# TensorE's up projections first and down projections last in the wave steps, and nine dense chunks of the fifth group moved ahead

## What is computed

```python
def reference(x, ...):
    h = adapter(x, language)                    # small two-layer adapter and layer norm
    for i in range(4):                          # four Mamba layers
        n = layer_norm(h)
        xs, z = split(n @ W_in.T)
        u = silu(causal_conv4(xs) + cb)
        dt, B, C = split(u @ W_x.T);  dt = softplus(dt @ W_dt.T + b_dt)
        # for t:  state = exp(dt*A)*state + dt*B*u ;  y = sum over 16 states of state*C
        h = h + ((y + u * D) * silu(z)) @ W_out.T
    x = x + h
    # dense mixture: 8 experts and a shared one, every token through all nine
    m = (1 - sg) * sum_e gate_e * ((silu(x @ Wg[e]) * (x @ Wu[e])) @ Wd[e]) + sg * shared(x)
    # sparse mixture: top 2 of 8 experts by m @ wg, 1024 slots each, exact gelu
    return x + combine(dispatch(m))
```

## Time and profile before

| | us |
|---|---|
| median of 3 runs (2779.27 to 2789.38) | 2783.77 |
| profiled execution | 2781.01 |
| its span, first to last instruction | 2779.3 |
| iterations 0 to 14, from the first scan at 122.1 | 853 |
| iterations 15 to 30 | 1142.8 |
| iteration 31 and the end of the wave, to 2195.0 | 77 |
| dense phase, to TensorE's last down | 393 |

### The profile page before, as it was taken

The page is one execution under the profiler, slowest core; times in us unless marked ns, Lnnn a source line. Parts: engine busy times, 40 slices in busy tenths (PEclk is TensorE's granted clock), DMA queues, the critical chain, the costliest instruction groups (busy, mean ns, idle before and its releaser), DMA issues. The chain is left out here.

```text
span 2779.3 us, 22910 instructions
## 1 busy us (share of the span) xinstructions
PE 2392.7 (86%) x6062; PEld 1060.4 (38%) x6062; DVE 2064.0 (74%) x2022; ACT 1565.8 (56%) x2430; POOL 2048.5 (74%) x1268
## 2 busy tenths in 40 slices
PE   5389989989988889888898889888987799999586
PEld 3133333333333333333333333333332344444364
DVE  4389999999999988888888888888888433333221
ACT  2367776776777666666666666666664232322132
POOL 3379999999998878888888888888888422231176
PEclk9799999999999999999999999999998899999798
DMA  7444564455445766666666566666665500000154
GB/s 198 163 150 152 199 221 176 157 197 193 154 143 188 258 210 215 217 224 210 213 220 212 197 217 216 215 215 219 217 210 182 185 11 17 27 16 8 40 118 73
DMA packets 217995, 462.38 MB, mean 166 GB/s; under 512 B 29644, under 2 KB 111506, under 8 KB 217746
## 3 DMA queue, kind: packets, MB, share of 16 engines
q1 hardware_dynamic: 204178, 449.66, 48.4%
q0 software_dynamic: 11264, 7.98, 1.9%
q10 hardware_dynamic: 2432, 3.38, 0.3%
HBM read 437.51 MB, written 23.99 MB: 166 GB/s over the span
## 5 line engine op out<-in xcount | busy, mean ns | idle before, releaser
L831 DVE TENSOR_TENSOR_SCAN hh<-dA,psdB 128x1024 f32<-128x1024 f32 x512 | 1167.6, 2284 | 97.3 <-ACT dA L735 39.1
L906 POOL TENSOR_TENSOR gg<-hh,Clo 128x1024 f32<-128x1024 f32 x408 | 960.8, 2358 | 213.6 <-DVE hh L831 209.5
L556 PE MATMUL psY<-gg,ident 128*128 128x512 f32 x1708 | 877.3, 640 | 88.9 <-POOL gg L910 56.4
L735 ACT ACTIVATE dA<-dt,Acur 128x508 f32<-128x508 f32 x1024 | 664.7, 708 | 20.6 <-DVE hh L831 20.2
L556 PEld LDWEIGHTS psY<-gg,ident 128*128 128x128 f32 x1708 | 328.9, 202 | 546.9 <-issue 374.7
L820 DVE TENSOR_TENSOR psdB<-psT,Blo 128x1024 f32<-128x1024 f32 x395 | 483.2, 1223 | 59.8 <-ACT psT L706 44.6
L1296 DVE TENSOR_TENSOR ac<-sg,d_bank 128x512 f32<-128x512 f32 x144 | 99.0, 687 | 244.2 <-PE d_bank L1146 227.0
L537 PE MATMUL psW<-xnT,wcur 128*128 128x512 f32 x512 | 236.5, 604 | 39.2 <-ACT u L672 19.7
L906 POOL TENSOR_TENSOR gg<-hh,late 128x1024 f32<-128x1024 f32 x104 | 243.9, 2362 | 19.1 <-PE psY L556 18.9
L1195 ACT ACTIVATE sg<-d_bank 128x512 f32<-128x512 f32 x144 | 86.0, 597 | 262.1 <-PE d_bank L1142 262.1
L1050 POOL TENSOR_TENSOR xw<-x1T,wbc 128x512 f32<-128x512 f32 x36 | 37.5, 1044 | 257.0 <-PE d_bank L1146 244.1
(11 more groups left out here) (171 smaller groups left out, 2965.8 us busy)
## 6 DMA issues: line engine op xcount, KB each, us to landing
Blo<-rows SPq DMA_DIRECT2D x280, 512.0 KB, 5.3
Clo<-rows SPq DMA_DIRECT2D x280, 512.0 KB, 4.8
late<-rows SPq DMA_DIRECT2D x104, 512.0 KB, 7.8
wcur<-taps_l SPq DMA_DIRECT2D x32, 512.0 KB
disp<-fw SPq DMA_DIRECT2D x16, 528.0 KB, 8.3
dx<-disp SPq DMA_DIRECT2D x16, 528.0 KB, 6.3
fw<-in_Wg SPq DMA_DIRECT2D x32, 256.0 KB, 5.1
fw<-in_Wu SPq DMA_DIRECT2D x32, 256.0 KB, 4.9
```

The source lines that it names most:

```text
L556: ins = pe.matmul(psY[:, :], lhsT=ident[:, :], rhs=gg[k % NGB][:, j, :], start=False, stop=(k % NK == NK - 1 and j == last - 1))
L735: ins = act.activation(dA[k % NDA][:, j, :, 1:T], dt[i % 2][:, c, :, 1:T], ACT.Exp, scale=Acur[i % 2][:, s:s + 1])
L831: dve.tensor_tensor_scan(out=hh[k % NHB][:, :, :].rearrange("p c t -> p (c t)"), data0=dA[k % NDA][:, :, :, :].rearrange("p c q t -> p (c ...
L906: ins = pool.tensor_tensor(gg[k % NGB][:, :, :], hh[k % NHB][:, :, :], tile(Clo, Chi, slot(i, s)), ALU.mult)
```

## The change

- In the wave TensorE's order in a step becomes: sum (steps 7 and 15 only), ups, transposes, gates, work, downs, skip, sum.
- New tables for the five pieces of a chunk. Each up is now two steps ahead of its product, but for the last two, which are one ahead. The first gate stands at step 5 of the iteration before and was at step 8. The transposes move from step 4 to 3.
- `gate1` on GpSimd moves from step 3 to step 1; `PAIRED` drops step 1 and takes step 3. The row copy `bcdt` on ScalarE moves from step 10 to step 8.
- The stream has nine chunks more (`NSTR` = 153): a fifth group's first nine chunks run in iteration 31 and, for the last ups, products and downs, in a loop after it. Group 4 gets its residual, store and transposes in iteration 30. Iteration 31 has silus of its own with a preload of the table. The sum so far is copied from `psD` to `part`, which lies where `xc` was a tensor of its own, and `fw` is kept.
- The dense phase starts at chunk 9 of group 4, with x taken transposed from `h_res`, experts 2 and 3 from `fw`, and `part` put into `psD` by one identity matmul. It loads no x and makes no transposes for group 4. Weights are loaded from expert 4 on and then round. The residual of group 5 comes after one chunk, behind x loaded as the seventh DMA. Routing in group 4 moves to chunks 10 and 23.

```diff
+NSTR = NDF * NST + NB
-SUM_FIRST = (7, 14, 15)
-ACT_AT = {1: ["params", "dtu1", "norm"], 2: ["turn0"], 4: ["sums1", "x0"], 5: ["x1"], 6: ["z0"], 7: ["z1", "silu"], 10: ["bcdt", "turn1"], 11: ["dt0"],
+SUM_FIRST = (7, 15)
+ACT_AT = {1: ["params", "dtu1", "norm"], 2: ["turn0"], 4: ["sums1", "x0"], 5: ["x1"], 6: ["z0"], 7: ["z1", "silu"], 8: ["bcdt"], 10: ["turn1"], 11: ["dt0"],
-POOL_AT = {3: ["gate1"], 6: ["rstd"], 10: ["dt"], 11: ["dtu"], 12: ["gate0"]}
-G_AT = [-8, -7, -6, -5, -4, -3, -2, 0, 1]
-C_AT = [-3, -2, -1, 0, 1, 2, 3, 5, 6]
-U_AT = [5, 7, 9, 10, 12, 13, 15, 17, 19]
-V_AT = [7, 9, 10, 12, 13, 15, 17, 19, 21]
-D_AT = [9, 9, 10, 12, 13, 15, 17, 19, 21]
-T_AT = 4
+POOL_AT = {1: ["gate1"], 6: ["rstd"], 10: ["dt"], 11: ["dtu"], 12: ["gate0"]}
+G_AT = [-11, -9, -7, -6, -5, -4, -2, 0, 1]
+C_AT = [-5, -3, -2, -1, 0, 1, 3, 5, 7]
+U_AT = [5, 7, 9, 11, 13, 15, 17, 19, 20]
+V_AT = [7, 9, 11, 13, 15, 17, 19, 20, 21]
+D_AT = [9, 10, 12, 14, 16, 18, 20, 21, 22]
+T_AT, X_AT = 3, 9
-PAIRED = [0, 1, 2, 5, 7, 8, 9, 13, 14, 15]
+PAIRED = [0, 2, 3, 5, 7, 8, 9, 13, 14, 15]
...
                         if k in SUM_FIRST:
                             sum_states(i, k)
-                        for n in stream(D_AT, i, k):
-                            down(n)
                         for n in stream(U_AT, i, k):
                             up(n)
...
                         work(i, k)
+                        for n in stream(D_AT, i, k):
+                            down(n)
...
-                project(NIT - 1)
-                turn_back(NIT - 1)
+                for k in range(NSTEP):
+                    for n in stream(U_AT, NIT, k):
+                        up(n)
+                    for n in stream(D_AT, NIT, k):
+                        down(n)
+                    if k == 2:
+                        project(NIT - 1)
+                    if k == 4:
+                        turn_back(NIT - 1)
...
+                            if what == "silu" and i + 1 == NIT:
+                                silu_gates(i - FIRST)
+                                act.preload_act_table_set(LNEXP)
...
-                place_sum(NDF - 1)
                 copy_sums(NIT - 1, 1)
                 place_delta(NIT - 1)
                 added(NIT - 1)
+                act.wait_ge(downed, NSTR)
+                act.activation(K["part"][:, :], psD[:, :], ACT.Copy).then_inc(sum_ok, 1)
...
+        kept = {(0, e): (NDF * NE1 + e) % NXW for e in (NB // NF, NB // NF + 1)}
+        def first(h):
+            return NB if h == 0 else 0
...
+        def x_of(h):
+            return h_res[:, G * NDF:G * (NDF + 1), :] if h == 0 else x1T[h % 2][:, :, :]
...
-                load_x(0)
-                for e in range(NE1):
+                for e in [a % NE1 for a in range(NB // NF + 2, NB // NF + 2 + NE1)]:
...
-                    if e == 1:
+                    if e == NB // NF + 3:
                         load_x(1)
...
+                    if h == 0 and r == first(0):
+                        pe.matmul(psD[:, :], lhsT=ident[:, :], rhs=K["part"][:, :], start=True, stop=False)
...
-                transpose_x(0)
...
-                        if h + 1 < NDT and r == 4:
+                        if h + 1 < NDT and r == first(h) + 1:
                             residual(h + 1)
```

More of the change, by code:

```diff
@@ L287, in stream @@
 def stream(at, i, k):
-    return [NB * v + m for v in range(NDF * NF) for m in range(NB) if NSTEP * (FIRST + v) + at[m] == NSTEP * i + k]
+    return [NB * v + m for v in range(NDF * NF + 1) for m in range(NB) if NSTEP * (FIRST + v) + at[m] == NSTEP * i + k]
 def openings(at, i, k, lead):
-    return [n // NF for n in range(NDF * NST) if n % NF == 0 and NSTEP * (FIRST + n // NB) + at[n % NB] - lead == NSTEP * i + k]
+    return [n // NF for n in range(NSTR) if n % NF == 0 and NSTEP * (FIRST + n // NB) + at[n % NB] - lead == NSTEP * i + k]
 def pair(i, k):
@@ L347, in wave_phase @@
         spare = sb("spare", [128, 1])
-        xc = sb("xc", [128, G, D])
+        xc = K["part"][:, :].rearrange("p (q d) -> p q d", q=G)
         u = [sb(f"u{p}", [128, NH, TOK]) for p in range(2)]
@@ L515, in _ @@
                             load_updown(a)
-                sp.wait_ge(zeroed, 16 * 2 * NE)
+                a = NSTR // NF + 1
+                load_gate(a)
+                load_updown(a)
+                for b in (a - 1, a):
+                    sp.wait_ge(g_ld[b % NXW], 16 * (b // NXW + 1))
+                    sp.wait_ge(ud_ld[b % NXW], 32 * (b // NXW + 1))
             @block.tensor
@@ L601, in down @@
                         at_least(pe, sum_ok, n // NST)
-                    pe.matmul(psD[:, :], lhsT=fwd[:, e % NXW, f, :], rhs=sg[:, n % NSLG, :], start=(n % NST == 0), stop=(n % NST == NST - 1)).then_inc(downed, 1)
+                    pe.matmul(psD[:, :], lhsT=fwd[:, e % NXW, f, :], rhs=sg[:, n % NSLG, :], start=(n % NST == 0), stop=(n % NST == NST - 1 or n == NSTR - 1)).then_inc(downed, 1)
                 def work(i, k):
@@ L862, in _ @@
                             act_product(n)
+                for k in range(NSTEP):
+                    for n in stream(V_AT, NIT, k):
+                        act_product(n)
             @block.gpsimd
@@ L949, in _ @@
                 gate(NIT - 1, 1)
+                for k in range(NSTEP):
+                    for a in openings(U_AT, NIT, k, 2):
+                        scale(a)
 def dense_phase(nc, A, K, out):
@@ L1035, in _ @@
             def _(pool):
[L1036 removed]
+                pool.sem_inc(scaled, CR + NB // NF)
                 n = 0
@@ L1060, in scatter @@
                                                     tok[p][:, q, :], None, bounds_check=2 * NSLOT - 1, oob_is_err=False).then_inc(scat[p], 16)
-                for e in range(NXW):
+                for e in range(NB // NF, NB // NF + NXW):
                     scale(0, e)
@@ L1183, in ratio @@
                     act.activation(e2[:, :], diff[:, :], ACT.Exp).then_inc(exp_ok, 1)
-                copy_x(0)
                 for h in range(NDT):
-                    for r in range(NST):
+                    for r in range(first(h), NST):
                         n = NST * h + r
@@ L1273, in slots @@
                     dve.tensor_copy(idx[p][:, :, :], dest[:, :, :]).then_inc(slots_ok, 1)
-                residual(0)
                 for h in range(NDT):
-                    for r in range(NST):
+                    for r in range(first(h), NST):
                         n = NST * h + r
-                        if h + 1 < NDT and r == 4:
+                        if h + 1 < NDT and r == first(h) + 1:
                             residual(h + 1)
@@ L1481, in mega @@
             "wr": sb(ctx, "wr", [128, NE]),
+            "part": sb(ctx, "part", [128, TOK]),
+            "fw": sb(ctx, "fw", [128, 3 * NXW, F]),
         }
```

89 lines of the change are left out of this document (52 added, 37 removed).

## The result

The changed kernel took 2718.7 us (median of 4 runs, 2713.4 to 2719.3) beside 2782.3 for the kernel before: 0.9764 of its time, 95% interval 0.9741 to 0.9787, or 63.5 us less. The prediction said 2695 within 2652 to 2735, 88.8 less than its 2783.8. So the sign and the range held, and the gain is a quarter to a third smaller than forecast. The profiled run took 2718.9 (span 2717.1).

The account below looks back on a forecast made before the run. No engine was full; a four-engine loop (70.5 us) with VectorE's floor (64.6) behind it bound iterations 15 to 30. Terms -61.2 - 3 + 0.5 + 4.5 - 26.3 = -85.5 from 2781.0 gave 2695, range 2652 to 2735.

Parts of the forecast that it names:

- Both waits go: Iterations 15 to 30: ScalarE's 2.56 us wait for gate1 before copying z0 and TensorE's 2.12 ahead of z1 vanish.
- These 4.3 us of waits go: Iterations 15 to 30: with ups first and downs last, VectorE's 4.3 us of waits for up projections an iteration vanish.
- The loop: 64.3 and 2.5 of half clock: Iterations 15 to 30: four-engine loop of 64.3 us; 2.5 for TensorE's half clock on top of the 64.6 floor gives 66.8.
- VectorE's floor: Iterations 15 to 30: an iteration without VectorE's 6.0 us of named waits takes 64.6 us.
- the forecast of 1081.6: Iterations 15 to 30 together: 12 at 66.8 and 4 at 70.0 us, 1081.6 against 1142.8, so -61.2.
- First gate: 3.2, bounds 0 and 8: Iterations 18, 22, 26, 30: the first gate waits for the transposed x, about 4.8 us idle, adding 3.2 to the loop.
- a wait of like length stays, and I keep its half-clock cost: TensorE, iterations 15 to 30: the 2.96 us wait ahead of dt0 goes, but a similar one ahead of sum 7 stays.
- Iterations 0 to 14: -3, bounds +4 and -12: Iterations before the dense chunks: gate1 and the row copy come sooner, with smaller waits of the same kinds; -3 us.
- Iteration 31, drain and dense phase: +0.5, +4.5, -26.3: Kernel's end: products in iteration 31 +0.5, longer drain +4.5, dense phase with nine chunks fewer and an earlier start -26.3 us.
- The rule: Trainium skill: weight-load busy share (38% in iteration 20) and arithmetic rate, not matmul busy time, show TensorE's limit; much room.
- the floor rival: Whole kernel: TensorE never drops to half level, iterations 64.6 us and those four 67, total 2653; chance 0.17.
- The slower rival: Stage: a gate copy waiting for a late down delays the psT copy; iterations 74.2 us, total about 2801; chance 0.06.

Follow-up runs that it names:

- filled: The changed kernel with three matmuls of zeros added ahead of sum 7 in iterations 15 to 31; 2708.1 us, 0.9721 of the kernel before.
- short_early_old_gates: short_early with gate matmuls, gate copies and transposes back at the steps of the kernel before (first gate at step 8); 2643.3 us, 0.9481 of the kernel before.
- short_early: The changed kernel with the two ups only one step ahead of their products moved from steps 19 and 20 to 5 and 6; 2663.1 us, 0.9559.
- row_copy_late: The changed kernel with ScalarE's row copy back at step 10, ahead of the psT copy; 2700.6 us, 0.9682 of the kernel before.
- order_undone: The changed kernel with TensorE's downs ahead of ups again and sum 14 ahead of x0; 2733.5 us, 0.9816 of the kernel before.
- gate1_late: The changed kernel with GpSimd's gate1 back at step 3 and that step's pair sum back at step 1; 2765.2 us, 0.9921 of the kernel before.
- tail_alone: The kernel before with only the nine chunks in the drain and the new dense phase; 2764.1 us, 0.9932 of the kernel before.
- early_rows_late_busy: early_rows_late with three matmuls of zeros added ahead of dt0 in every stage iteration; 2639.5 us, 0.9474 of the kernel before.
- early_rows_late: short_early_old_gates with ScalarE's row copy back at step 10; 2685.4 us, 0.9632 of the kernel before.

## Why the prediction was right in range and wrong in the stage

*gate1 at step 1: "Both waits go."* Right, and worth 44 us. In the stage no copy of sz waits for GpSimd, and no z1 for it.

*Order: "These 4.3 us of waits go."* This is the step that failed. The wait at step 10 went, but VectorE's waits for ups fell only from 88.0 to 83.8 us in the stage. The text itself said that the last two products stand one step behind their ups, counted TensorE's matmuls from sum 7 to the down of step 2 to see when the last gate is copied, and stopped there. That count was good: 45.2 and a wait of 1.6, where the trace has 47.9 us (1346.09 to 1394.02) with a wait of 1.45 and 1.7 of half level in it. Two matmuls on, at 49.6 us, it meets the product of step 20, and 38.6 of the 83.8 us stand there. Two steps between up and product weren't enough either: 24.1 us stand at step 11, which filled brings to 3.8, so most of those come with the half level behind sum 7.

*The loop: 64.3 and 2.5 of half clock.* The iterations of short_early_old_gates are 64.5, beside 64.6 for VectorE's floor and 64.3 for the loop through silus and decays. With 10.3 us of named waits of VectorE in 16 iterations it is the floor that binds there; no run shows that loop as the limit. In the changed kernel the next loop was ahead of both. The stage can be shared out in measured terms: 16 x 64.4 (short_early's plain iterations) is 1030; 3.8 more (68.2 of filled less 64.4) in 15 iterations, 57, less 1.6 for iteration 15; the first gates 4.0 each, 16; the half level behind sum 7, 11. That makes 1113 for the 1112.8 measured. It closes because all terms but the first come from filled and from the changed kernel's distance to it, so it proves nothing; it says where to look. Of the 3.8, 1.7 are the output projection at the half level, 26 in 15 iterations, and 2.1 are the seam, 31 (estimates). So the half level costs some 37 us, and the 40 forecast (2.5 x 16) were about right. The first gates were forecast at 13. The seam stood at 0, and its 31 us are what the forecast of 1081.6 lacks.

*First gate: 3.2, bounds 0 and 8.* 4.0 by filled. TensorE's wait is 4.05 us (forecast 4.8), and it goes with the old gates' steps. The price isn't fixed: in row_copy_late a like wait of 3.58 us stands in iterations of 68.2 and 69.6, beside plain ones of 68.4.

```profile
1479.23 2.04 PE L593 MATMUL psdB<-h_res,fw 128*128 128x512 f32 x2 [4.05 <-ACT h_res L754]
1481.06 1.91 PE L608 MATMUL psT<-late,fw 128*128 128x512 f32 x2
```

*Row copy: "a wait of like length stays, and I keep its half-clock cost".* The wait stayed (3.41 ahead of sum 7 for 2.96 ahead of dt0), and behind it the clock fell in some iterations and not in others. But its place decided the cost: moved behind sum 7, the slow matmuls lie on the loop, and the part loses 18 to 23 us.

*Iterations 0 to 14: -3, bounds +4 and -12.* -11.5, at the far bound. order_undone shows the source (854.7 us, where gate1_late and row_copy_late keep 841.6 and 840.1): x0 ahead of sum 14, which the text had seen for the stage ("covers its 1.70 us wait") and not counted here.

*Iteration 31, drain and dense phase: +0.5, +4.5, -26.3.* -0.6, +5.0, -27.5, and tail_alone bears the sum out within its interval. In the dense phase the wait for x is there as said; the third product, second of the last row, starts at about 2169.1, 9.9 us after the phase began at 2159.2 (forecast 7.3 and 2):

```profile
2164.11 0.69 DVE L1344 TENSOR_TENSOR ac<-sg,d_bank 128x512 f32<-128x512 f32 x1 [9.31 <-PE d_bank L1194]
2167.90 0.69 DVE L1272 TENSOR_TENSOR x1g<-xin,h_res 128x512 f32<-128x512 f32 x1 [3.10 <-DMA xin<-in_x]
2168.51 1.28 DVE L1344 TENSOR_TENSOR ac<-sg,d_bank 128x512 f32<-128x512 f32 x2
```

*The rule and the rivals.* The two kernels that reach the floor rival's time meet its condition, TensorE hardly ever or never at the half level; the changed one doesn't. Whether that condition alone would have been enough no run shows, for neither of the two has the seam. That TensorE has much room, as the rule had it by weight loads (the Trainium skill, Perfetto Trace Analysis, Identifying the Most-Contended Engine), the traces don't bear out: weight loads are busy for 26.0 of 64.5 us, 40%, but the prediction's 70 matmuls at 0.86 us are 60 of them, and 78 us hang on one wait of 2.8 us an iteration. The rule's other measure, the arithmetic rate, wasn't worked out. The slower rival, a psT copy behind a late down, didn't come: 0.6 us in the stage.

What each part is worth, by the differences of the ratios (times 2785 us; minus is faster with the part):

| part | with the changed tables | with the early gaps and old gates |
|---|---|---|
| gate1 at step 1 | -44 | -78 |
| order | -15 | -57 |
| row copy at step 8 | +23 | -42 |
| new steps of ups, products, downs | -2, within the noise | |
| the tail | -19 | |

They don't add up to the whole, and the signs aren't fixed. What stays open: the gates' new steps with the changed kernel's other tables weren't tried alone, and how the 3.8 us at the seam split between the product's place and the clock is an estimate.

## What to carry to other kernels

When a loop is found and cut, follow the work that is left over one step beyond the point where your own argument ends, and ask who waits there; here the next loop was nearly as long as the first, 68.1 us for 70.5. Where an engine is nearly full, a step that is only one behind its input belongs where that engine is ahead, and a change should be tried in its place among the others, for its sign can depend on them. A long wait can cost more in the matmuls behind it than in itself: look at which instruction stands behind it, split it, or fill it.

## What the hardware showed that was not expected

- More work made the kernel faster, twice: 51 matmuls of zeros brought 11 us in filled, and 48 brought 44 in early_rows_late_busy.
- The length of an idle stretch of TensorE didn't tell what the clock did behind it. In short_early_old_gates 2.01 us (iteration 20) and 3.21 us (iteration 15) were followed by matmuls at the full level, and 2.30 us (iteration 22) by two at the half level, 1.2 GHz. In other kernels single stretches of 2.34, 2.70 and 3.40 us were followed by the half level, and so was one of 1.45 us in the changed kernel (0.51 over the next 3.5 us), but not in short_early.
- The same wait doesn't always cost the same. Behind 2.70 us the six sum passes took 4.87 us in one iteration and 3.46 in the next; behind 3.41 us, in iteration 20 of the changed kernel, sum and up took 1.12 and 1.02, and behind 3.40 one iteration later 2.07 and 1.91. So a wait's price in clock is a range, here from 0 to over 3 us: from dt0 to the up behind the sums are 7.9 us in iteration 24 of early_rows_late and 4.6 in early_rows_late_busy.
